# Linear attention with routed experts on one core: projections regrouped, normalisation spread over three engines, ranks and register loads in new places

## The chip, the core and the metric

The kernel runs on one NeuronCore of a Trainium2 chip. The metric is the device time of one execution in microseconds, as the median of several executions. The core has TensorE (PE, matrix products, with its weight loads shown as PEld), VectorE (DVE), ScalarE (ACT), GpSimd (POOL) and SyncE (SP); each has its own instruction stream, runs it in order, and waits for others through semaphores.

## What is computed

The input `x` is 8 x 256 tokens of 128 features: 2048 tokens, 16 tiles of 128. The output is the input plus two branches over its layer norm:

```python
xn = (x - mean) / sqrt(var + 1e-5)
# branch 1: linear attention, 16 heads of 8 features, inside each batch of 256 tokens
Q, K, V = xn @ Wq, xn @ Wk, xn @ Wv
Qf, Kf = elu(Q) + 1, elu(K) + 1
out1 = (Qf @ (Kf.T @ V)) / (Qf @ sum(Kf) + 1e-6)   # per head
out1 = out1 @ Wo
# branch 2: top 2 of 8 experts for every token
probs = softmax(xn @ gate_w.T + gate_b)
out2 = sum over the two largest: probs[e] * (relu(xn @ w1[e] + b1[e]) @ w2[e] + b2[e])
x + out1 + out2
```

All is fp32. Each expert is 128 x 256 and 256 x 128.

## The kernel before, in words

The order of the work is written out by hand, as one list of steps for each engine; there is no scheduler. A *part* is a group of tiles that are loaded and normalised together (`PARTS`: tiles 0-1, 2-3, 4-7, 8-11, 12-15), a *block* is four tiles, a *batch* two tiles.

**Normalisation.** DVE takes the statistics of each part (`statistics`, L593), ACT the square root (`deviation`, L485), DVE the reciprocal (`inverse_deviation`, L601). The tiles themselves are normalised by DVE, ACT or POOL as `NORM_DVE`, `NORM_ACT` and `NORM_POOL` say (L103 to L105). PE transposes a part (`transpose_x`, L880), and ACT copies the result to SBUF (`copy_xT`, L500).

**Projections.** `project_kv` (L913) makes keys and values of one batch: a product of ones with one row, which adds 1 to the keys, two tiles of keys, two of values, in one PSUM bank, of which three take turns. ACT takes the exponential of the keys (`exp_k`) and copies the values (`copy_v`), DVE finishes the keys (`finish_k`, L726). `make_logits` (L897) makes the gate's logits of four tiles: a product of one row for the bias and four products of 8 columns. `project_q` (L950) makes queries of a block. An fp32 product of one tile is two matmul instructions in the profile, each with its own weight load.

**Ranks.** DVE finds the two best experts of each token in PSUM (`top_two`, L617), and which of the 28 pairs of experts they are (`find_pair`, L626). `rank_rows` (L932) counts on PE how many tokens of each pair come before; after the fourth, DVE makes each token's row number from it (`pair_starts`, `places`, L649 to L669), `slot_done` says so. POOL then writes every tile's rows to DRAM at these row numbers (`dispatch`, L429), sixteen indirect DMAs, each behind the gates of its rows (`gate_values` on POOL for tiles 0 to 7, `late_gates` on DVE for the others). SP reads the sorted rows back when all sixteen have landed (`load_rows`, L355). `visits`, `order_visits` and `make_table` turn the pair counts into a table of at most 59 visits, each of one expert to one tile of sorted rows.

**Attention.** `keys_values` (L972, into one PSUM bank), `mask_kv` (L739), `numerator` (L987), `divide` (L746), `transpose_att` (L1002), `project_out` (L1010) and `residual` (L763) run over the four blocks.

**Experts.** PE transposes the sorted rows (`transpose_rows`, L1023) and makes 59 visits: `first_product` (L1037), a relu on ACT (L538), `second_product` (L1054). DVE adds the bias (`take_y`, L773) and adds to the tile's sum (`accumulate`, L781). PE, DVE and SP read each visit's addresses from the table into registers, `LOADS` visits at a time, each by a TENSOR_LOAD (`offsets_of`, L328). POOL adds every finished tile to the output by an indirect DMA (`give_back`, L452), which waits for the number of visits that can reach the tile: 8, 16, 23, 28, 33, 37, 40, 43 for the first eight tiles and then two more for each.

## Time and profile before

| | |
|---|---|
| median of three executions | 121.21 us (121.0 to 124.61) |
| the profiled execution, its own time | 120.49 us |
| its span in the profile | 118.7 us |
| mean granted TensorE clock | 0.938 of full speed |
| busy: PE, PEld, DVE, ACT, POOL | 105.1, 94.5, 70.9, 58.6, 48.6 us |

The span is the time from the first to the last instruction; about 1.8 us of the execution's time lie around it. PE busy counts a matmul from its start to its modelled end, and these overlap, so the distance between starts is the better measure of cost. "issue" as a releaser means that the engine waited for nothing that the profile shows.

### The profile page before, as it was taken

The page shows a single profiled execution, that of the slowest core. Times are in us where ns is not written, and L with a number is a line of the kernel's source. Part 1 is how long each engine was busy: PE and PEld are TensorE (multiplying, and loading weights), DVE is VectorE, ACT ScalarE, POOL GpSimd, SP SyncE. Part 2 cuts the span into 40 slices and gives each one's busy share as a digit, 9 for nine tenths or more (in the row PEclk, how much of TensorE's full clock was granted, in tenths as well). Part 3 has the DMA queues.
Part 4 walks back from the last instruction along what each step waited for, and adds up shares of the span by engine and source line. Part 5 has one row for each costly group of instructions (what it writes and reads, how often), then busy time and mean ns, then how long its engine had stood idle before and what let it go on. Part 6 is the DMA issues. An engine that isn't in the chain of part 4 may idle for free.

```text
span 118.7 us, 3131 instructions
## 1 busy us (share of the span) xinstructions
PE 105.1 (89%) x787; PEld 94.5 (80%) x787; DVE 70.9 (60%) x292; ACT 58.6 (49%) x169; POOL 48.6 (41%) x62
## 2 busy tenths in 40 slices
PE   6969799999999999777999999999999999999200
PEld 6957677565768799666999999999999999999100
DVE  0878953949717478943376665656657566575510
ACT  1556945232245203214866677766766776666000
POOL 5004221007777778411000500405405556878770
PEclk9999999755599999999999999999999999999975
DMA  3997000000211851499675575766776777883422
GB/s 93 289 370 315 3 6 0 0 0 24 71 50 50 223 165 57 105 239 315 186 182 136 136 160 145 168 162 144 171 166 151 166 183 170 140 161 34 42 25 25
DMA packets 16514, 15.51 MB, mean 131 GB/s; under 512 B 1778, under 2 KB 16114, under 8 KB 16370
## 3 DMA queue, kind: packets, MB, share of 16 engines
q1 hardware_dynamic: 13248, 12.88, 38.3%
q0 software_dynamic: 2816, 2.18, 12.3%
q10 hardware_dynamic: 434, 0.27, 0.7%
q8 instruction: 7, 0.11, 0.4%
q14 instruction: 9, 0.07, 0.2%
HBM read 12.09 MB, written 3.23 MB: 129 GB/s over the span
## 4 chain that ended last, share of the span: by engine, by line
PE 36%; issue 28%; POOL 19%; ACT 4%; DVE 3%; DVEq 2%; POOLq 2%; DMA 2%
POOL out L457 19%; PE banks L960 4%; PE banks L925 4%; PE banks L983 4%; PE banks L877 4%; PE banks L998 3%; PE banks L928 3%; PE banks L909 2%; PE banks L1019 2%; DVEq L330 2%; DMA out<-res 2%; ACT xrow L497 2%; POOLq L115 2%; ACT xT L503 2%; PE banks L893 1%
## 5 line engine op out<-in xcount | busy, mean ns | idle before, releaser
L543 ACT ACTIVATE h<-banks,w_now 128x128 f32<-128x128 f32 x118 | 36.9, 365 | 17.6 <-PE banks L1050 17.6
L457 POOL DMA_INDIRECT out<-acc,token x16 | 25.1, 1569 | 34.3 <-DVE acc L786 33.1
L1050 PE MATMUL banks<-xsT,w_now 128*128 x236 | 36.4, 278 | 0.7 <-ACT xsT L536 0.7
L1063 PE MATMUL banks<-w_all,h 128*128 x236 | 36.1, 277 | 0.0
L1050 PEld LDWEIGHTS banks<-xsT,w_now 128*128 128x128 f32 x236 | 30.9, 192 | 1.2 <-issue 1.1
L1063 PEld LDWEIGHTS banks<-w_all,h 128*128 128x128 f32 x236 | 31.0, 192 | 0.3
L778 DVE TENSOR_TENSOR y<-banks,w_all 128x128 f32<-128x128 f32 x59 | 17.2, 292 | 20.7 <-DVE acc L786 11.3
L786 DVE SCALAR_TENSOR_TENSOR acc<-y,xs,acc 128x128 f32 x59 | 20.7, 351 | 0.8 <-DVE y L778 0.6
L442 POOL DMA_INDIRECT sorted_dram<-xrow,slot x16 | 15.5, 971 | 10.4 <-DVE slot L669 6.1
L531 ACT COPY attT<-banks 128x512 f32<-128x512 f32 x4 | 2.3, 586 | 9.1 <-PE banks L1007 9.1
L526 ACT ACTIVATE qf<-banks,minus_one 128x512 f32<-128x512 f32 x4 | 2.8, 688 | 8.2 <-PE banks L960 8.2
L925 PE MATMUL banks<-wkvg_f,xT 128*128 128x128 f32 x32 | 6.7, 341 | 0.0
L521 ACT ACTIVATE kf<-banks,minus_one 128x256 f32<-128x256 f32 x8 | 3.8, 473 | 4.7 <-PE banks L928 4.7
L925 PEld LDWEIGHTS banks<-wkvg_f,xT 128*128 128x128 f32 x32 | 5.0, 223 | 1.2 <-issue 0.4
L928 PE MATMUL banks<-wkvg_f,xT 128*128 128x128 f32 x32 | 5.8, 312 | 0.0
L1019 PE MATMUL banks<-wo_f,attT 128*128 128x128 f32 x32 | 4.4, 280 | 1.5 <-ACT attT L531 1.5
L596 DVE BATCH_NORM_STATS2 stats<-x_tok 128x6 f32<-128x128 f32 x16 | 3.6, 281 | 3.5 <-DMA x_tok<-in_x 3.5
L983 PEld LDWEIGHTS banks<-vext,kf 128*128 128x128 f32 x32 | 5.2, 227 | 0.5 <-issue 0.5
L983 PE MATMUL banks<-vext,kf 128*128 128x144 f32 x32 | 5.6, 326 | 0.0
L877 PE MATMUL banks<-ones 128*128 128x128 f32 x22 | 4.6, 399 | 1.1 <-POOL ones L385 1.1
L960 PE MATMUL banks<-xT,wq_f 128*128 128x512 f32 x8 | 5.5, 769 | 0.0
L1019 PEld LDWEIGHTS banks<-wo_f,attT 128*128 128x128 f32 x32 | 3.9, 191 | 1.9 <-DVE res L765 1.9
(100 smaller groups left out, 117.3 us busy)
## 6 DMA issues: line engine op xcount, KB each, us to landing
w_now<-in_w1b SPq DMA_DIRECT2D x59, 129.0 KB, 2.6
w_all<-in_w SPq DMA_DIRECT2D x1, 1536.0 KB, 8.4
out<-res SPq DMA_DIRECT2D x4, 256.0 KB, 4.5
xs<-sorted_dram SPq DMA_DIRECT2D x3, 276.0 KB, 5.2
x_tok<-in_x SPq DMA_DIRECT2D x3, 256.0 KB, 4.7
xs<-sorted_dram SPq DMA_DIRECT2D x2, 138.0 KB, 2.3
x_tok<-in_x SPq DMA_DIRECT2D x2, 128.0 KB, 2.5
sorted_dram<-xrow,slot POOLq DMA_INDIRECT x16, 2.4
```

The costliest lines, as they stand in the source:

```text
L442: nc.gpsimd.indirect_dma_start(out=sorted_dram, out_offset=bass.IndirectOffsetOnAxis(ap=slot[:, t:t + 1], axis=0), in_=xrow[:, t, :], in_o ...
L457: nc.gpsimd.indirect_dma_start(out=out_rows, out_offset=bass.IndirectOffsetOnAxis(ap=token[:, s:s + 1], axis=0), in_=acc[:, s * D:(s + 1) ...
L543: nc.scalar.activation(h[:, i % NH, c, :], h_ps[i % NHP][:, c * P:(c + 1) * P], ACT.Relu, bias=w1_now[:, i % NW, H + c:H + c + 1]).then_in ...
L778: nc.vector.tensor_tensor(y[:, i % 2, :], y_ps[i % NYP], w2_all[:, bass.ds(woff + KC * D, D)], ALU.add).then_inc(y_done, 1)
L786: nc.vector.scalar_tensor_tensor(out=mine, in0=y[:, i % 2, :], scalar=xs[:, bass.ds(goff, 1)], in1=mine, op0=ALU.mult, op1=ALU.add).then_i ...
L925: nc.tensor.matmul(kvp_ps[b][:, r, 0:D], xT[:, (R * b + r) * P:(R * b + r + 1) * P], wkvg_f[:, 0:D], start=False, stop=(r == R - 1))
L928: last = nc.tensor.matmul(kvp_ps[b][:, r, D:KV], xT[:, (R * b + r) * P:(R * b + r + 1) * P], wkvg_f[:, D:KV], start=True, stop=True)
L960: nc.tensor.matmul(q_ps[k], wq_f[:], xT[:, blk_cols(k)], start=False, stop=True).then_inc(q_done, 1)
L983: last = nc.tensor.matmul(kv_ps[:, 256 * b:256 * b + NV], kf[:, t, :], vext[:, t, :], start=(r == 0), stop=(r == 1))
L1019: last = nc.tensor.matmul(wo_ps[k][:, j * P:(j + 1) * P], attT[:, t * P:(t + 1) * P], wo_f[:], start=True, stop=True)
L1050: last = nc.tensor.matmul(h_ps[i % NHP][:, c * P:(c + 1) * P], w1_now[:, i % NW, c * P:(c + 1) * P], xsT[:, bass.ds(toff, P)], start=True, ...
L1063: last = nc.tensor.matmul(y_ps[i % NYP], h[:, i % NH, c, :], w2_all[:, bass.ds(woff + c * D, D)], start=(c == 0), stop=(c == KC - 1))
```

## The change

- Logits leave their own products. `project_vg` multiplies a tile of xT by the columns of V and of the gate together (136 columns); a bank holds two tiles, and four banks take turns. The one-row product for the gate's bias is gone: DVE adds the bias when it copies the logits to SBUF (`take_logits`), for two tiles at a time, and the bias is loaded to all partitions. `top_two` now works on two tiles and reads SBUF.
- Keys are made for four tiles at a time (`project_k`, one bank), and `exp_k` and `finish_k` take four tiles in one instruction.
- Normalisation: DVE has one tile less in parts 2 and 4, POOL takes tiles 7 and 15; `statistics(3)` and `(4)` stand before the part ahead of them is finished.
- The list of every engine is new: on DVE all pairs are found ahead of `shares`, `finish_k` and the late gates; on PE the rank products stand between the value products, and attention's steps are reordered after `numerator(1)`; ACT switches to the exponential's table after `copy_v(3)`.
- `LOADS` is 10 instead of 8, and PE's first two register loads stand before `project_out(2)` and `project_out(3)`.

```diff
-    LOADS, AHEAD = 8, 3
+    LOADS, AHEAD = 10, 3
...
-    NORM_DVE = [[0, 1], [2], [4, 5], [], [12, 13]]
-    NORM_ACT = [[], [3], [6, 7], [8, 9], [14, 15]]
-    NORM_POOL = [[], [], [], [10, 11], []]
+    NORM_DVE = [[0, 1], [2], [4], [], [12]]
+    NORM_ACT = [[], [3], [5, 6], [8, 9], [13, 14]]
+    NORM_POOL = [[], [], [7], [10, 11], [15]]
...
-        q_ps = [banks[:, (k + 1) % 2, :] for k in range(NBLK)]
-        kvp_ps = [banks[:, 2 + b % 3, :].rearrange("p (r n) -> p r n", r=R) for b in range(B)]
+        q_ps = [banks[:, i, :] for i in (2, 3, 4, 2)]
+        vg_ps = [banks[:, (2, 3, 4, 6)[b % 4], 0:R * (D + E)].rearrange("p (r n) -> p r n", r=R) for b in range(B)]
+        k_ps = [banks[:, i, :].rearrange("p (t d) -> p t d", t=4) for i in (7, 1, 0, 7)]
...
+            normalise(2)
             normalise(3)
+            normalise(4)
             fill_rows()
...
-            nc.scalar.dma_start(gate_bias[:], gate_b).then_inc(gate_b_in, 16)
+            nc.scalar.dma_start(gate_bias[:], gate_b.partition_broadcast(P)).then_inc(gate_b_in, 16)
...
             deviation(2)
+            normalise(2)
+            deviation(3)
+            normalise(3)
+            copy_xT(2)
+            deviation(4)
             copy_v(0)
-            deviation(3)
-            normalise(2)
-            normalise(3)
-            deviation(4)
-            copy_xT(2)
+            normalise(4)
+            copy_xT(3)
             copy_v(1)
+            copy_xT(4)
+            copy_v(2)
+            copy_v(3)
             exponentials()
-            copy_xT(3)
-            normalise(4)
+            exp_gates(0)
+            exp_gates(1)
+            for b in range(4, B):
+                copy_v(b)
             exp_k(0)
-            exp_gates(0)
-            copy_xT(4)
             exp_k(1)
...
+            def take_logits(b):
+                ts = slice(R * b, R * b + R)
+                dve.wait_ge(vg_done, b + 1)
+                if b == 0:
+                    dve.wait_ge(gate_b_in, 16)
+                nc.vector.tensor_tensor(logits[:, ts, :], vg_ps[b][:, :, D:D + E],
+                                        gate_bias[:].unsqueeze(1).to_broadcast([P, R, E]), ALU.add
+                                        ).then_inc(logits_done, 1)
...
+            def project_vg(b):
+
+                if b == 0:
                     pe.wait_ge(wkvg_in, 16)
+                pe.wait_ge(xT_copied, parts_with(R * b + 1))
+                if b >= 4:
+                    pe.wait_ge(v_done, b - 3)
+                for r in range(R):
+                    last = nc.tensor.matmul(vg_ps[b][:, r, :], xT[:, (R * b + r) * P:(R * b + r + 1) * P],
+                                            wkvg_f[:, D:KVG], start=True, stop=True)
+                last.then_inc(vg_done, 1)
+
+            def project_k(k):
+
+                if k == 0:
+                    pe.wait_ge(ones_set, 2)
+                elif k < 3:
+                    pe.wait_ge(xT_copied, k + 3)
+                else:
+                    pe.wait_ge(kf_done, 1)
+                nc.tensor.matmul(k_ps[k], ones_bf[0:1, 0:P], ones_bf[0:1, :].rearrange("p (t d) -> p t d", t=4),
                                  start=True, stop=False)
                 for j in range(4):
+                    t = 4 * k + j
+                    last = nc.tensor.matmul(k_ps[k][:, j, :], xT[:, t * P:(t + 1) * P], wkvg_f[:, 0:D],
                                             start=False, stop=(j == 3))
+                last.then_inc(k_done, 1)
...
```

The new lists of steps after the change, DVE from the statistics of part 3 on, then PE:

```
DVE: statistics(3), inverse_deviation(2), normalise(2), statistics(4), inverse_deviation(3),
     take_logits(0), top_two(0), inverse_deviation(4), normalise(4), take_logits(1), top_two(1),
     find_pair(0), take_logits(2), top_two(2), choose(0), take_logits(3), top_two(3), find_pair(1),
     (take_logits, top_two)(4), (5), find_pair(2), (take_logits, top_two)(6), (7), find_pair(3),
     shares(0), choose(1), shares(1), choose(2), pair_starts, places(1), places(2), late_shift,
     choose(3), finish_k(0), late_gates, finish_k(1), finish_q(0), finish_k(2), visits, finish_k(3),
     order_visits, finish_q(1), keep_table, mask_kv(0), finish_q(2), finish_q(3), mask_kv(1),
     mask_kv(2), divide(0), mask_kv(3), ... as before
PE:  warm_up, transpose_x(0), (1), project_vg(0), (1), project_k(0), transpose_x(2),
     project_vg(2), (3), transpose_x(3), rank_rows(0), project_vg(4), transpose_x(4),
     project_vg(5), rank_rows(1), project_vg(6), (7), project_k(1), rank_rows(2), project_q(0),
     rank_rows(3), project_k(2), project_q(1), (2), project_k(3), keys_values(0), order_visits,
     project_q(3), make_table, keys_values(1), (2), numerator(0), (1), transpose_att(0),
     keys_values(3), project_out(0), transpose_att(1), numerator(2), project_out(1), numerator(3),
     transpose_att(2), register load, project_out(2), transpose_att(3), register load,
     project_out(3), then the experts
```

In the PE list of before, `keys_values(3)` stood ahead of `transpose_att(0)`, and `numerator(2)` ahead of `project_out(0)` and `transpose_att(1)`.

## Rows read from the trace of the kernel before

**Rows 1.** The chain in order of time, steps of PE: start, us, what

```profile
14.61 0.69 PE banks L944 x4
...
19.55 0.99 PE banks L909 x8
...
32.55 1.05 PE banks L960 x2
...
34.46 0.45 PE banks L928 x4
...
37.82 0.98 PE banks L983 x8
38.80 0.32 PE banks L959
```

**Rows 2.** Timeline, 53 to 55 us: the first visit

```profile
53.86 0.37 ACT L536 COPY xsT<-banks 128x256 f32<-128x256 f32 x1 [1.53 <-PE banks L1033]
...
54.71 1.15 PE L1050 MATMUL banks<-xsT,w_now 128*128 x8 [0.67 <-ACT xsT L536]
```

**Rows 3.** Timeline: the rows' way through DRAM, POOL, SP's queue, POOL

```profile
26.77 1.15 POOL L442 DMA_INDIRECT sorted_dram<-xrow,slot  x1 [5.83 <-DVE slot L669]
...
48.21 2.51 SPq L357 DMA_DIRECT2D xs<-sorted_dram  x5
...
50.56 0.18 POOL L449 CAST token<-xs 128x2 uint32<-128x2 f32 x1 [1.87 <-DMA xs<-sorted_dram]
```

**Rows 4.** Timeline, 85 to 114 us, the visits on DVE and PE, POOL's writes

```profile
85.77 0.29 DVE L778 TENSOR_TENSOR y<-banks,w_all 128x128 f32<-128x128 f32 x1 [0.49 <-DVE acc L786]
...
92.98 0.29 DVE L778 TENSOR_TENSOR y<-banks,w_all 128x128 f32<-128x128 f32 x1 [0.49 <-DVE acc L786]
...
96.26 0.61 PE L1063 MATMUL banks<-w_all,h 128*128 x4
...
97.86 0.29 DVE L778 TENSOR_TENSOR y<-banks,w_all 128x128 f32<-128x128 f32 x1 [0.21 <-PE banks L1063]
...
98.73 1.55 POOL L457 DMA_INDIRECT out<-acc,token  x1 [0.83 <-DVE acc L786]
...
113.88 1.55 POOL L457 DMA_INDIRECT out<-acc,token  x1 [0.30 <-issue]
```

**Rows 5.** The page's second part: TensorE's granted clock in 40 slices, in tenths

```profile
PEclk9999999755599999999999999999999999999975
```

**Rows 6.** Windows: length, busy us of PE, PEld, DVE, ACT, POOL, clock, DMA share, GB/s

```profile
18.00:22.00 4.00, 3.78 (x24) 2.32 (x23) 2.30 (x20) 1.76 (x6) 0.75 (x3) 1.00 0.00 0
...
28.00:32.00 4.00, 4.00 (x17) 3.65 (x16) 3.62 (x13) 1.31 (x3) 2.89 (x3) 0.50 0.16 53
```

**Rows 7.** Timeline, 10 to 16 us: POOL's scaling, a copy of xT, DVE's searches

```profile
10.46 0.61 POOL L394 TENSOR_TENSOR xrow<-x_tok,mean_var 128x256 f32<-128x256 f32 x1 [8.27 <-DVE rstd L604]
...
11.87 0.56 ACT L503 COPY xT<-banks 128x512 f32<-128x512 f32 x1
...
14.10 0.38 DVE L620 MAX8 top<-banks 128x8 f32<-128x8 f32 x4
...
15.08 0.17 DVE L632 TENSOR_SCALAR idxk<-idx 128x8 f32<-128x8 uint32 x1
```

**Rows 8.** Timeline, 25 to 30 us, DVE: the ranks and what follows

```profile
25.35 0.21 DVE L653 TENSOR_TENSOR_SCAN start_of<-ones,banks 128x28 f32<-128x28 f32 x1 [1.50 <-PE banks L944]
...
27.47 0.50 DVE L669 TENSOR_REDUCE slot<-picked 128x12 uint32<-128x336 f32 x1
27.89 0.21 DVE L710 TENSOR_REDUCE expsum<-expd 128x8 f32<-128x64 f32 x1
...
29.05 0.68 DVE L736 SCALAR_TENSOR_TENSOR qf<-qf,banks 128x512 f32<-128x512 f32 x1
```

**Rows 9.** Timeline, 42 us, DVE: the first division begins

```profile
42.17 0.23 DVE L750 TENSOR_SCALAR den<-banks 128x64 f32<-128x64 f32 x1 [0.18 <-PE banks L998]
```

**Rows 10.** Register loads, line 330, PE's queue: count, ns min/median/max, first and last start

```profile
L330 PEldq TENSOR_LOAD <-table x16: 587/592/1649, 52.8 to 107.6; - x16
```

More of the change, by code:

```diff
@@ L154, in linear_attention_with_pair_sorted_experts @@
         res = sb("res", [P, T, D])
+        logits = sb("logits", [P, T, E])
         top8 = sb("top8", [P, T, 8])
@@ L207, in linear_attention_with_pair_sorted_experts @@
         table_ps = banks[0:3, 5, P:P + NI]
-        logits_ps = [banks[:, 6 + g % 2, 0:4 * E].rearrange("p (t e) -> p t e", e=E) for g in range(NBLK)]
         kv_ps = banks[:, 6, :]
@@ L514, in copy_v, with exp_k @@
             def copy_v(b):
[L515 to L521 removed]
+                act.wait_ge(logits_done, b + 1)
+                nc.scalar.copy(vext[:, R * b:R * b + R, 0:D], vg_ps[b][:, :, 0:D]).then_inc(v_done, 1)
+            def exp_k(k):
+                act.wait_ge(k_done, k + 1)
+                nc.scalar.activation(kf[:, blk_tiles(k), :], k_ps[k], ACT.Exp, bias=minus_one[:, 0:1]
                                      ).then_inc(kexp_done, 1)
@@ L795, in _ @@
             statistics(2)
+            statistics(3)
             inverse_deviation(2)
             normalise(2)
-            statistics(3)
+            statistics(4)
             inverse_deviation(3)
-            statistics(4)
+            take_logits(0)
             top_two(0)
-            find_pair(0)
             inverse_deviation(4)
             normalise(4)
+            take_logits(1)
+            top_two(1)
+            find_pair(0)
+            take_logits(2)
+            top_two(2)
             choose(0)
-            top_two(1)
+            take_logits(3)
+            top_two(3)
             find_pair(1)
+            take_logits(4)
+            top_two(4)
+            take_logits(5)
+            top_two(5)
+            find_pair(2)
+            take_logits(6)
+            top_two(6)
+            take_logits(7)
+            top_two(7)
+            find_pair(3)
+            shares(0)
             choose(1)
-            shares(0)
-            finish_k(0)
             shares(1)
-            finish_k(1)
-            top_two(2)
-            find_pair(2)
             choose(2)
-            top_two(3)
-            find_pair(3)
-            late_shift()
-            choose(3)
             pair_starts()
@@ L822, in _ @@
             places(2, slice(4, T))
+            late_shift()
+            choose(3)
+            finish_k(0)
             late_gates()
+            finish_k(1)
             finish_q(0)
@@ L827, in _ @@
             finish_k(3)
+            order_visits()
             finish_q(1)
-            order_visits()
-            finish_k(4)
+            keep_table()
             mask_kv(0)
-            keep_table()
-            finish_k(5)
             finish_q(2)
-            finish_k(6)
+            finish_q(3)
             mask_kv(1)
-            finish_k(7)
-            finish_q(3)
             mask_kv(2)
@@ L1100, in _ @@
             numerator(1)
+            transpose_att(0)
             keys_values(3)
-            transpose_att(0)
-            numerator(2)
             project_out(0)
             transpose_att(1)
+            numerator(2)
+            project_out(1)
             numerator(3)
-            project_out(1)
             transpose_att(2)
+            toffs = offsets_of(mybir.EngineType.PE, 1, 0, T_TOP)
             project_out(2)
             transpose_att(3)
+            woffs = offsets_of(mybir.EngineType.PE, 0, 0, W_TOP)
             project_out(3)
```

134 lines of the change are left out of this document (46 added, 88 removed).

## The prediction, made before the changed kernel was built

> **What bounds the kernel now.** I read the chain of waits in order of time first. Up to 5.7 us it is TensorE's warm-up, then normalising and ACT's copies of xT alternate; from about 12.5 us to the end of attention nearly every piece is a product on TensorE [rows 1]. After that, "issue" and POOL's additions alternate: the experts run on TensorE at 0.89 us a visit, and the chain ends on POOL. The first visit's product starts at 54.71 us, 0.85 us after ACT has begun its copy of the sorted rows; that copy needs 0.37 us, so about 0.45 us are the register load in front [rows 2]. The other way to the first visit goes through DRAM: POOL's sixteen writes start at 26.77 us, the read is issued at 48.21, and POOL holds the first rows at 50.56 us [rows 3]. TensorE came to transposing them only after 53.3 us, so this way has some 2.8 us to spare, and attention sets the start. What moves the start of the visits moves the end as much, for the 59 visits are there in both. In the tail DVE lags: the bias addition of visit 43 starts at 97.86 us, though TensorE's product for it was over about 1.15 us earlier (the product at 96.26 and 0.45 us), and from the eighth write on POOL is nearly back to back, 15.15 us for 8 writes [rows 4]. Last, the clock: it falls to half at about 22.2 us and is back at about 32.4 [rows 5, 6], ten microseconds in which TensorE is the chain.
>
> **The change on TensorE.** Removed: four one-row products (0.32 us each by the like one of the queries) and 32 passes of 8 columns, 0.99 us for eight; that is 4 x 1.31 = 5.2 us [rows 1]. A batch's values and logits are four passes of 136 columns. They lie between four of 128 in 0.45 us and, of 144, eight in 0.98 us: 0.45 to 0.49, I take 0.47 [rows 1]. Keys of a block are a one-row product of 512 columns, 0.32, and eight passes, 0.89: 1.2 us, against 2 x 0.65 before.
>
> One rule speaks against a gain here. The 8-column pass takes 0.12 us, as much as one of 128 columns [rows 1]. The Trainium skill (TensorE: Matmul & The Clock Gate, Back-to-back issue gap) lets a small matmul's gap sink to about 25 ns, but says for pairs with a weight load that both instructions set the spacing. By the floor alone the 32 passes would give back, as an estimate, only 0.8 us instead of 4; the trace agrees with the second half of the rule.
>
> **Step 1, up to the ranks.** `statistics(3)` ahead of part 2's scaling delays that scaling by 0.6 us, but DVE has one tile less, and ACT takes its tiles of part 2 before it waits for part 3's deviation: part 2 is normalised at about 9.8 us instead of 11.0. ACT then does part 3's two tiles and copies xT of part 2. That copy began at 11.87 us [rows 7]; now about 11.45, and the next products start at 12.0. POOL's single tiles in parts 2 and 4 were not traced: two operations of 128 columns each, between half of the one of 256 columns and all of it, so 0.6 to 1.2 us [rows 7]. I take 0.7, which lies inside ACT's two tiles (0.88) and costs nothing; at 1.2 it costs 0.3. From 12.0 to the end of the last rank product TensorE has six value products, 2.8; eight transposes, 0.9; four rank groups of about 0.7 [rows 1], 2.8; keys of one block, 1.2; queries of one block, 0.32 + 1.05, 1.4: 9.1 us. One wait: `rank_rows(0)` needs the first pairs, and TensorE's next products and part 4's transposes are queued behind it. On DVE the first pairs follow the deviation of part 4 (12.25, behind ACT's copy), 0.65 us of scaling, one batch's logits, and the pair: 14.3 us, where TensorE is free at 13.4: 0.9 us. Sum: 12.0 + 9.1 + 0.9 = 22.0 us, against 25.3 before (the scan that waited for it starts at 25.35 [rows 8]): 3.3 us earlier.
>
> DVE in this stretch has more to do. Eight `take_logits` were not traced either; the nearest small operations take 0.17 us [rows 7] and 0.21 [rows 8], so 0.2 each with its handover. `top_two` and its searches take 0.98 us for four tiles [rows 7]; as two pairs 1.06, from SBUF perhaps 0.1 less. So 0.7 us a batch, 1.7 us more over all. From 14.3 on DVE's own sum (six batches 4.2, three pairs 2.1, a `choose` 0.2, then both `shares` and two `choose` 1.1) ends at 21.9 us, level with TensorE. An error of 0.1 us a batch therefore costs up to 0.8 us. ACT: the table load moves from an idle stretch (12.7 us) behind `copy_v(3)`; loaded with its first use in 1.5 us, values 4 to 7 follow to 21.0, `project_q(0)` needs value 4 at about 19.9 and starts at 20.2. Hidden, with 0.3 us of cover. The bias's broadcast load is a different access on ACT's queue; all loads of this size landed within 5 us, it is read at 10.6 us: hidden.
>
> **Step 2, ranks to the first division.** This stretch becomes DVE's. In order: scan and both places 2.65 (25.35 to 27.97 [rows 8]); late shift and choice 0.35; late gates 1.25 (27.89 to the finish at 29.05 and its overlap); four `finish_k` of 512 columns and four `finish_q`, 0.65 each at the spacing behind a row of 0.68 [rows 8], 5.2; visits 0.95; order and table 1.0, a wait of 0.2 in it; two masks 0.8. Sum 12.2, to 34.2 us. TensorE's second `keys_values` waits for `keep_table` and the first mask, but its 0.98 us lies beside `finish_q`. Behind 34.2 come `keys_values(2)` and `numerator(0)`, 0.98 each [rows 1]: the first division starts at 36.1 us against 42.17 [rows 9]: 6.1 earlier, 2.8 more than step 1 gave, much of it the clock, which I leave at full here. `order_visits` on TensorE waits for DVE's visits (29.8), and `project_q(3)` stands behind it; still in time for `finish_q(3)` at 33.0.
>
> POOL's first write, after one `places` (1.15) and handover, starts at 23.5, the whole way is 3.3 us earlier [rows 3]; POOL's own gates for blocks 0 and 1 follow `shares` at 21.3 and end at 23.3, just in time. The first rows are there at 47.3 us.
>
> **Step 3, the divisions.** It gives something back. `keys_values(3)` now stands behind `transpose_att(0)`, which waits for the first division, and DVE's next step, `mask_kv(3)`, waits for it: 0.44 + 0.98 + 0.05 = 1.5 us instead of 0.4. `numerator(2)` stands behind `transpose_att(1)`: DVE waits 0.9 us more where it waited for nothing. The first register load, 1.65 us where its kind takes 0.59 [rows 10], lies behind `transpose_att(2)`, beside ACT's copy of 0.6: it costs between 0 and 0.6 us. I take 12.6 us from first division to the last product's end, where 11.2 stood: 1.4 us lost, with 0.9 and 2.0 as ends. Attention ends at 48.7 us, 1.4 us after the first rows are there.
>
> **Step 4, the first visit.** Without the register load in front it follows ACT's copy at once, 0.95 us behind attention's end instead of 1.35: 0.4 us gained [rows 2]. It starts at 36.1 + 12.6 + 0.95 = 49.65 us, 5.1 earlier. DVE's three loads are ten values each now, not traced; their length for eight is the same few tenths whatever the line, and they lie beside TensorE's first two visits. Between nothing and 0.3 us.
>
> **Step 5, the visits.** DVE's cycle with 8 visits is 85.77 to 92.98, 7.21 us [rows 4]: five visits of 0.80 and three of 1.075, each of these with one register load in it. TensorE's eight are 7.15. So DVE never catches up. With 10 it is seven of 0.80 and three of 1.075, 8.8, against 8.93: the lag of 1.15 us at visit 43 should shrink to about 0.3, and POOL starts its closing run 0.8 earlier. The run itself has 1.55 + 0.30 us a write [rows 4], 14.8 at best against 15.15. I take 0.9 us for both, 0.3 to 1.2 as ends. The rest is worth nothing, for POOL holds the end.
>
> **The sum.** -3.3 - 2.8 + 1.4 - 0.4 - 0.9 = -6.0 us at full clock. The last unknown is the clock.
>
> **The clock.** It fell, from 2.4 to 1.2 GHz, after a stretch with TensorE at work 3.78 of 4 us, in short passes, with weight loads busy 2.32 us, and it came back after one with weight loads for 3.65 us [rows 6]. The change makes 14 to 22 us denser, but between 8.5 and 12 us TensorE has only 0.85 us of keys and 0.44 of transposes, less than in the stretch that ended in the fall. So I expect a fall again, at about 12 us, now followed by dense work, and so shorter. While it lasts each 0.111 us pass costs 0.22, but the wait for the first pairs takes up the first microsecond. A slow stretch of 3.4 to 7 us costs 1.0 to 2.2; I take 1.2. Result: 120.49 - 6.0 + 1.2 = 115.7 for the profiled execution, and since the median was 0.7 above that execution, 116.4 us.
>
> The Trainium skill (TensorE: Matmul & The Clock Gate, Why this matters for your kernels) ties a fall to TensorE standing idle between bursts. No idle gap stood before this fall, so the trace doesn't agree. By the rule alone the changed kernel, whose longest gap is 1.75 us, would not fall; that is rival A.
>
> **Rivals.** A: the clock stays up. For it: the empty passes of 8 columns are gone, and 14 to 22 us is dense. Against it: the thin stretch before 12 us. 120.49 - 6.0 + 0.7 = 115.2 us. B: the clock is down as long as before, 10 us from 12 to 22. Then only half of step 1's 9.1 us is done in it: the ranks end 4.2 us later, at 26.1, and everything behind. 119.4 us. For it: the same length before [rows 5]. C: attention is quicker than I add up and the rows' way binds: visits start at 47.3 + 0.95 = 48.25, 1.4 earlier still, and the time is 113.8. Against it: 1.4 us of spare. D, slower: the clock falls twice, at 12 and again in the divisions (34 to 46 us), where every step of TensorE is on the chain: `keys_values(2)` and (3), two numerators, three transposes, some 5 us at full clock. That costs 4.2 + 4.7 against 6.0, so 124.1 us; it decides from about 6 us of loss on, some 14 slow microseconds in places that TensorE bounds. For it: DVE's stretch of step 2 leaves TensorE idle 3 to 4 us of 28 to 35. Against it: no fall in the like divisions of before [rows 5].
>
> **Chances.** Forecast 0.42, its own range 115.3 to 117.9; A 0.25; B 0.17; C 0.08; D 0.08. The range 114.4 to 119.8 leaves out C, D and little else. 2% of 121.21 are 2.4 us, about what a measurement here tells from no change: below 118.8 lie the forecast, A, C and a part of B, 0.80; within 2% the rest of B and of the near cases, 0.13; above, 0.07.
>
> **What would show it.** Right: no products of 8 columns; the scan after the ranks near 22 to 23.5 us; the first division near 37; DVE idle some 1.5 us ahead of the fourth mask; the first visit at 50 to 51 us with no "issue" in front; DVE close behind TensorE at visit 43. Wrong: a slow clock beyond 20 us, DVE late with the fourth pair, the first visit after 53 us, or the first rows later than attention's end.

## The result and the profile after

The changed kernel takes 137.51 us (136.91 to 138.33, 4 runs), the kernel before in the same session 121.1 (119.86 to 124.61, 4 runs): ratio 1.140, 95% interval 1.127 to 1.153, slower. The forecast was 116.4, range 114.4 to 119.8, with a chance of 0.07 for slower. The profiled execution took 138.33 us, where the working came to 115.7; its span is 136.5. The kernel before has medians of 123.91, 124.36 and 121.48 us in the sessions of the experiments, since some executions there, of the changed versions too, had a lower mean clock; the ratios leave those out.

| us of the span | forecast | before | after |
|---|---|---|---|
| scan behind the ranks | 22.0 (clock aside) | 25.35 | 23.46 |
| first division | 36.1 (clock aside) | 42.17 | 40.67 |
| first rows on POOL | 47.3 | 50.56 | 49.69 |
| first visit's product | 50.85 with 1.2 for the clock | 54.71 | 55.99 |
| from there to the end of the span | 63.1 | 64.0 | 80.5 |

By the second last row 5.1 us of the miss of 22.6 had come up before the visits, by the last 17.4 in them. (The first rows came 2.4 us later than forecast, but TensorE was not waiting for them.) The visits do what they did before and their lines are as short as before, so the first question is what stands between them. DVE's timeline, columns start, length, engine, line, operation, operands, and in brackets the idle time ahead with its releaser:

```profile
64.48 0.29 DVE L786 TENSOR_TENSOR y<-banks,w_all 128x128 f32<-128x128 f32 x1 [0.21 <-DVE acc L794]
...
68.08 0.29 DVE L786 TENSOR_TENSOR y<-banks,w_all 128x128 f32<-128x128 f32 x1 [2.19 <-PE banks L1072]
...
70.87 0.29 DVE L786 TENSOR_TENSOR y<-banks,w_all 128x128 f32<-128x128 f32 x1 [2.20 <-issue]
...
73.68 0.29 DVE L786 TENSOR_TENSOR y<-banks,w_all 128x128 f32<-128x128 f32 x1 [2.23 <-PE banks L1072]
...
92.60 0.29 DVE L786 TENSOR_TENSOR y<-banks,w_all 128x128 f32<-128x128 f32 x1 [2.19 <-PE banks L1072]
```

Three visits in a row have 2.2 us of nothing ahead of their bias addition, where [rows 4] had 0.49. The same three stalls begin again at 92.60, twenty visits later: 24.52 us for twenty, 1.23 a visit, against 7.21 for eight, 0.90, before. The releaser in the bracket names TensorE twice, but only because its product came last before a long gap. What DVE does in it is in the chain of waits:

```profile
64.71 0.46 PE banks L1072 x4
65.89 1.97 DVEq L332
68.67 1.98 DVEq L332
71.45 2.00 DVEq L332
74.21 0.71 PE banks L1072 x4
```

DVEq is DVE's sequencer, L332 the register load. TensorE has gaps of its own there:

```profile
66.72 0.71 PE L1059 MATMUL banks<-xsT,w_now 128*128 x4 [1.56 <-issue]
...
70.98 0.71 PE L1072 MATMUL banks<-w_all,h 128*128 x4 [1.34 <-issue]
```

And the view of one source line, L332, by queue (count, shortest, median and longest in ns):

```profile
L332 DVEq TENSOR_LOAD <-table x18: 1059/2078/2407, 52.0 to 120.1; - x18
L332 PEldq TENSOR_LOAD <-table x12: 1078/2279/2453, 49.4 to 116.7; - x12
L332 SPq TENSOR_LOAD <-table x6: 953/1514/2091, 33.1 to 108.7; - x6
```

Before, TensorE's had a median of 592 ns [rows 10]. Ten values cost not 10/8 of that but 1.06 to 1.08 us in one half of the loads and 2.0 to 2.45 in the other. In order of time they alternate: the groups that begin at visit 0, 20 and 40 are the short ones, those at 10, 30 and 50 (nine values) the long ones. The group at visit 0 is an exception: its first loads on TensorE took 1.28 and 2.41 us, DVE's first 2.41.

Ahead of the visits these first loads show: TensorE's last output product starts 1.67 us late behind its load of 2.41 us, and DVE's last residual stands 4.05 us behind its first three. TensorE's two in one line of the view:

```profile
L332 PEldq TENSOR_LOAD <-table x2: 1277/1844/2411, 49.4 to 51.5; - x2
```
```profile
54.03 1.13 PE L1028 MATMUL banks<-wo_f,attT 128*128 128x128 f32 x8 [1.67 <-issue]
```
```profile
56.70 0.69 DVE L773 TENSOR_TENSOR res<-banks,x_tok 128x512 f32<-128x512 f32 x1 [4.05 <-issue]
```

The clock fell before the visits as well, and twice, where before there was one stretch [rows 5]. The page's second part, and windows of 4 us (columns as in [rows 6]):

```profile
PEclk9999599999559999999999999995999999599995
```
```profile
14.00:18.00 4.00, 4.00 (x24) 3.16 (x24) 3.60 (x31) 1.15 (x4) 0.95 (x7) 0.68 0.00 0
...
34.00:38.00 4.00, 3.36 (x14) 3.04 (x14) 1.11 (x3) 0.00 (x0) 3.03 (x4) 0.50 0.62 145
38.00:42.00 4.00, 3.61 (x20) 3.39 (x18) 1.72 (x5) 0.00 (x0) 3.08 (x4) 0.69 0.52 173
```

The second stretch lies in `keys_values(1)` and (2) and the first numerators, where nearly every step of TensorE is on the chain. The later dips, at 92 and 116 us, come behind the gaps that the long loads leave.

Theory R, from here on: the register loads make the loss of the visits, and a load is long where its values begin on a column that isn't a multiple of four. The 2.41 us above don't fit it, for that load begins on column 0; in other versions too an engine's first loads take longer than later ones of the same size (up to 1.65 us before, 1.25 on TensorE in e1, 1.97 in e11), and no run shows why. One rival: a load is long when it holds more than eight values, wherever it begins. Another: the loads only cover a wait of another kind (the clock, the new order), and the visits would be slow with short loads too.

### The profile page after: what moved, and what is told of

The parts are those of the page before. It is cut to its first block, busy times and chain, and to the rows that moved or that the text cites. A ratio compares the mean times of both kernels' runs of the same rounds, so it can differ in the third digit from the quotient of the medians.

```text
span 136.5 us, 3023 instructions
## 1 busy us (share of the span) xinstructions
PE 106.4 (78%) x743; PEld 94.6 (69%) x743; DVE 71.8 (53%) x294; ACT 57.5 (42%) x165; POOL 50.5 (37%) x66
## 3 DMA queue, kind: packets, MB, share of 16 engines
q0 software_dynamic: 2816, 2.18, 10.9%
## 4 chain that ended last, share of the span: by engine, by line
PE 58%; DVE 13%; issue 9%; DVEq 5%; DMA 4%; ACT 4%; POOL 2%; POOLq 1%; SPq 1%
PE banks L1059 19%; PE banks L1072 18%; DVEq L332 4%; PE banks L990 4%; DMA x_tok<-in_x 4%; PE banks L921 3%; PE banks L1005 3%; PE banks L1028 2%; DVE stats L597 2%; ACT h L547 2%; POOL out L459 2%; PE banks L1014 2%; DVE acc L794 2%; PE banks L968 2%; PE banks L953 1%
## 5 line engine op out<-in xcount | busy, mean ns | idle before, releaser
L547 ACT ACTIVATE h<-banks,w_now 128x128 f32<-128x128 f32 x118 | 36.9, 365 | 33.2 <-PE banks L1059 33.0
L1059 PE MATMUL banks<-xsT,w_now 128*128 x236 | 38.5, 288 | 7.0 <-issue 6.0
L1072 PE MATMUL banks<-w_all,h 128*128 x236 | 38.4, 288 | 3.8 <-issue 2.2
L1059 PEld LDWEIGHTS banks<-xsT,w_now 128*128 128x128 f32 x236 | 32.7, 201 | 8.2 <-issue 8.2
L1072 PEld LDWEIGHTS banks<-w_all,h 128*128 128x128 f32 x236 | 32.5, 200 | 5.5 <-issue 5.5
L990 PE MATMUL banks<-vext,kf 128*128 128x144 f32 x32 | 6.8, 374 | 1.5 <-DVE kv L749 1.5
L921 PE MATMUL banks<-wkvg_f,xT 128*128 128x136 f32 x32 | 5.6, 315 | 1.5 <-ACT xT L507 1.5
L893 PEld LDWEIGHTS banks<-ones 128*128 128x128 f32 x22 | 4.8, 331 | 1.1 <-POOL ones L387 1.1
L1005 PE MATMUL banks<-kv,qf 128*128 128x144 f32 x32 | 5.4, 325 | 0.0
L773 DVE TENSOR_TENSOR res<-banks,x_tok 128x512 f32<-128x512 f32 x4 | 2.7, 686 | 4.6 <-issue 4.0
L1005 PEld LDWEIGHTS banks<-kv,qf 128*128 128x128 f32 x32 | 5.2, 230 | 0.0
```

The source lines that it names most:

```text
L547: nc.scalar.activation(h[:, i % NH, c, :], h_ps[i % NHP][:, c * P:(c + 1) * P], ACT.Relu, bias=w1_now[:, i % NW, H + c:H + c + 1]).then_in ...
L893: last = nc.tensor.matmul(warm_ps, ones[:], ones[:], start=True, stop=True)
L921: last = nc.tensor.matmul(vg_ps[b][:, r, :], xT[:, (R * b + r) * P:(R * b + r + 1) * P], wkvg_f[:, D:KVG], start=True, stop=True)
L990: last = nc.tensor.matmul(kv_ps[:, 256 * b:256 * b + NV], kf[:, t, :], vext[:, t, :], start=(r == 0), stop=(r == 1))
L1005: last = nc.tensor.matmul(num_ps[k][:, j // 2, (j % 2) * NV:(j % 2 + 1) * NV], qf[:, t * P:(t + 1) * P], kv[:, t // 2, :], start=True, sto ...
L1059: last = nc.tensor.matmul(h_ps[i % NHP][:, c * P:(c + 1) * P], w1_now[:, i % NW, c * P:(c + 1) * P], xsT[:, bass.ds(toff, P)], start=True, ...
```

## The experiments

**Eight values again, all else as changed (e1), and ten values in the kernel before (e2).**

```
-    LOADS, AHEAD = 10, 3
+    LOADS, AHEAD = 8, 3        # e1, in the changed kernel; e2 is 8 to 10 in the kernel before
```

> The changed kernel with one edit taken back: 8 values per register load instead of 10. Theory R (a load costs by its values and by where it begins: eight that begin on a multiple of four are taken together in 0.59 us, every other value alone in about 0.23 us): all loads are back to 0.59 us, the visits take the 64 us from the first product to the span's end that they took before, and the first product comes about 1 to 1.5 us earlier than the 55.99 of the changed kernel, since the load of 2.41 us in front of the last output product shrinks; some 118.5 to 120.5 us in all. Rival F (the new order of the front is what costs): still above 130 us.

> The kernel before with 10 values per register load and nothing else of the change. Theory R: loads of 1.07 and 2.3 us by turns, and the visits take the 80.5 us from first product to the end that they take in the changed kernel, 16.5 more than before: 136 to 139 us. Rival F: within 2 us of the kernel before.

e1: 120.61 us (118.63 to 121.45), ratio 0.988 (0.947 to 1.028). e2: 139.45 (136.07 to 142.38), the kernel before beside it 123.91. From the first product to the end of the span e1 takes 64.3 us, e2 80.5 (58.5 to 139.0), the changed kernel's own figure. So this one constant makes 16.2 us of the visits' loss, in either kernel, and no wait of another kind is needed. e2's time lies just above the 136 to 139 expected. The line of the loads in e1, then in e2:

```profile
L332 PEldq TENSOR_LOAD <-table x16: 588/595/1245, 49.3 to 108.1; - x16
```
```profile
L330 PEldq TENSOR_LOAD <-table x12: 1077/2256/2449, 56.0 to 119.5; - x12
```

**The place, with the count kept (e3), and the count, with the place mended (e4).** e3 is the kernel before, eight values a load, the table moved by two columns. e4 is the changed kernel with ten values a load, each group on a column that is a multiple of twelve; DVE's copy of the table is two operations instead of one.

```
 e3:     table = sb("table", [3, NI + 2], I32)
...
-             table[row:row + 1, i:min(i + LOADS, NI)], ...
+             table[row:row + 1, i + 2:min(i + LOADS, NI) + 2], ...
 e4:     PITCH = 12
...
-             table[row:row + 1, i:min(i + LOADS, NI)], ...
+             table[row:row + 1, i // LOADS * PITCH:i // LOADS * PITCH + min(LOADS, NI - i)], ...
```

> The kernel before, 8 values per load, but the table begins two columns later, so that every load begins at 2 modulo 8 columns. Theory R: no eight lie together from a multiple of four, so each load is eight single values, about 1.85 us instead of 0.59; three loads on VectorE per eight visits cost 1.26 us more each, seven times over: some 20 to 25 us more, 141 to 146 us. Rival L (it is the count: beyond eight values a load falls to a slow way, wherever it begins): 0.59 us and 121 us as before.

> The changed kernel with 10 values per load, but each group of ten begins at a multiple of twelve columns of the table, so always on a multiple of four. Theory R: every load of ten is about 1.07 us, none 2.3; the three groups that had 2.3 us lose 3 x 1.25 us each on VectorE, so 10 to 12 us less than the changed kernel, 125 to 128 us. Rival L: no change against the changed kernel, 137 us.

e3: 146.39 us (146.16 to 149.2), ratio 1.211 (1.172 to 1.249). e4: 122.84 (122.44 to 125.98), ratio 1.017 (0.982 to 1.051). The loads of e3, then of e4:

```profile
L330 DVEq TENSOR_LOAD <-table x24: 742/1844/3127, 50.2 to 135.2; - x24
```
```profile
L333 DVEq TENSOR_LOAD <-table x18: 857/1064/1677, 48.3 to 105.6; - x18
L333 PEldq TENSOR_LOAD <-table x12: 854/1082/1280, 45.6 to 103.5; - x12
```

Eight values take 1.84 us where they begin two columns off, three times their 0.59; ten on a good column take 1.06, and none takes 2 us. Both missed their expected times: e3 lies 0.4 us above 146, and e4 is 14.7 us under the changed kernel where 10 to 12 were expected. The rule of more than eight falls, R stands. In e3 1.84 / 8 is 0.23 us a value; its groups of three, the shortest, took 0.74, 0.25 a value. But R was not complete: with good columns for all, the visits of e4 still take 69.2 us (51.36 to 120.6), 4.9 more than those of e1.

**Twelve values (e8).** This tells whether the good load goes by single values or in steps.

```
-    LOADS, AHEAD = 10, 3
+    LOADS, AHEAD = 12, 3
```

> The changed kernel with 12 values per load; every group begins on a multiple of four. Theory R leaves open how the quick way is cut. If it takes four values at a time: 3 x 0.30 = 0.9 us for twelve. If it takes eight and then single values: 0.59 + 4 x 0.23 = 1.5 us. If it needed a multiple of eight at the start: three of the five groups quick, two slow with 2.8 us. The time: 118 to 122 us in the first case, 123 to 127 in the second, above 128 in the third.

121.01 us (120.37 to 123.62), ratio 1.006 (0.998 to 1.014).

```profile
L332 DVEq TENSOR_LOAD <-table x15: 843/858/1535, 48.2 to 101.0; - x15
L332 PEldq TENSOR_LOAD <-table x10: 849/864/1330, 45.6 to 99.1; - x10
```

Twelve values take 0.86 us, less than ten (1.07) and as long as nine (0.86, the last groups of e4). Eight are 0.59: so the times are those of fours at some 0.29 us each, and what is left over costs about 0.24 a value: ten is 2 x 0.29 + 2 x 0.24 = 1.06. From a column off the fours the cost is that of single values: 10 x 0.23 = 2.3. The twelves begin on columns 0, 12, 24, 36 and 48, so a multiple of eight isn't needed. All slow groups here begin two columns past a multiple of four; an odd column was not tried.

With these lengths DVE's cycle can be added up as in the prediction, where a load of 0.59 made a visit 0.275 longer than 0.80, 0.32 less than its own length. Twelve values: 12 x 0.80 + 3 x 0.54 = 11.2 us, against 10.7 of TensorE, 2.5 us over the visits; measured (67.2 - 64.3) 2.9. Ten on good columns: 8.0 + 3 x 0.75 = 10.25 against 8.93 for ten visits, 7.8 us over all; measured 4.9. The cycle itself came as added up: DVE's loads of e4 start at 61.3 and, forty visits later, at 102.8, 10.4 us for ten. The base was too low: in e1 they go from 62.8 to 107.4 in 48 visits, 9.3 for ten and not 8.93. Ten as changed: three short loads and three long ones in twenty visits, 16 + 3 x 0.75 + 3 x 1.98 = 24.2; measured 24.52.

**Which engine's loads (e11, e12).** TensorE has ten values a load in e11 and eight in e12, DVE and SP the other number.

```
+    PE_LOADS = 10              # e11, with LOADS = 8; e12: 8, with LOADS = 10
...
-             table[row:row + 1, i:min(i + LOADS, NI)], ...
+             table[row:row + 1, i:min(i + (PE_LOADS if engine == mybir.EngineType.PE else LOADS), NI)], ...
```

> The changed kernel with ten values a load on TensorE, eight on DVE and SP. From the measured lengths TensorE's loads in the visits add up to 6 x 2.4 + 4 x 1.08 = 18.7 us instead of 14 x 0.59 = 8.3: 10.4 more. Theory R (the sequencer of each engine stands for its own load, and the engine with more to do bounds): 59 visits of 0.89 and 18.7 are 71.2 us, about 74.5 from the first product to the end of the span, where e1 has 64.3 and the changed kernel 80.5; the time is some 131 us. Rival: the loads cost on DVE alone, and this kernel is as fast as e1, 120 to 121 us.

> The changed kernel with ten values a load on DVE and SP, eight on TensorE. DVE's loads add up to about 9 x 2.2 + 6 x 1.07 = 26.2 us instead of 21 x 0.59 = 12.4. Theory R: 59 visits of 0.80 and 26.2 are 73.4 us, with the tail of 4 about 77 to 78 from the first product to the end of the span; about 134 us. Rival: the loads cost on TensorE alone, and this kernel is as fast as e1, 120 to 121 us. If the costs of the two engines simply added, e11 and e12 together would be 88 - 64 = 24 us over e1; the changed kernel is only 16 over it, so each alone must be over half of that.

e11: 134.36 us, e12: 139.19, one run each. From the first product to the end of the span 76.1 and 86.1. Over e1's 64.3 TensorE's loads alone cost 11.8 us and those of DVE with SP's 21.8, and the two don't add: both together, in the changed kernel, cost 16.2. e11's visits came near what Theory R had (74.5); its time is 3.4 us over the 131 expected, about half of it because its first visit starts at 56.54 us, 1.6 later than e1's (part 2 of x, tiles 4 to 7, came 1.1 us later there). e12 is 8 us over its 78. Its waits show why: while DVE stands for three loads in three visits TensorE, whose banks it hasn't read, stands too, and the clock falls; after that TensorE is late. Rows of e12, TensorE's timeline and two windows:

```profile
71.13 0.71 PE L1073 MATMUL banks<-w_all,h 128*128 x4 [1.64 <-DVE y L787]
...
73.27 1.06 PE L1073 MATMUL banks<-w_all,h 128*128 x4
```
```profile
68.00:72.00 4.00, 1.87 (x12) 1.50 (x12) 1.55 (x6) 1.28 (x4) 0.00 (x0) 1.00 0.62 124
72.00:76.00 4.00, 3.74 (x19) 3.75 (x20) 1.75 (x6) 1.25 (x4) 0.00 (x0) 0.57 0.15 38
```

A sum per engine is therefore a floor of the loss, not the loss. How the 8 us divide between the clock and the waiting was not taken apart. Against the changed kernel e12, with less to load, has 5.6 us more in the visits; its page has four slices at half clock in them before the last one, against two there. Two more slices of 3.4 us at half clock are, as an estimate, at most 3.4 us of the 5.6; the rest is open, and each has one profile here.

**The order of the divisions (e6).** On top of e1 the old order: `keys_values(3)` ahead of `transpose_att(0)`, `numerator(2)` ahead of `project_out(0)`, `numerator(3)` ahead of `project_out(1)`.

```
+            keys_values(3)
             transpose_att(0)
-            keys_values(3)
+            numerator(2)
             project_out(0)
             transpose_att(1)
-            numerator(2)
+            numerator(3)
             project_out(1)
-            numerator(3)
```

> The changed kernel with 8 values per load and, behind the second numerator, TensorE's steps in the order of before: the fourth keys_values ahead of the first transpose, the third numerator ahead of the first output product. Theory (as the prediction had it, 0.9 to 2.0 us lost by the new order): VectorE waits about 0.4 us instead of 1.7 for the fourth mask and not at all instead of 1.1 us for the third division; first division to last output product 1.5 to 2 us shorter, 1 to 2 us less in all than the same kernel in the new order. Rival: the waits move elsewhere in the stretch and nothing is gained.

118.97 us (118.33 to 119.88), ratio 0.991 (0.980 to 1.002). From the first division to the first visit e1 took 14.39 us (40.57 to 54.96), e6 12.26 (40.72 to 52.98): 2.1 less. The fourth mask waited 1.73 us in the changed kernel and 0.36 in e6, rows of the one and of the other:

```profile
44.00 0.46 DVE L749 TENSOR_TENSOR kv<-banks,cst 128x288 f32<-128x288 f32 x1 [1.73 <-PE banks L990]
...
47.69 0.23 DVE L758 TENSOR_SCALAR den<-banks 128x64 f32<-128x64 f32 x1 [1.13 <-PE banks L1005]
```
```profile
42.68 0.46 DVE L749 TENSOR_TENSOR kv<-banks,cst 128x288 f32<-128x288 f32 x1 [0.36 <-PE banks L990]
...
45.62 0.21 DVE L758 TENSOR_SCALAR den<-banks 128x64 f32<-128x64 f32 x1
```

**TensorE's first two loads, moved out of the end of attention (e9).** On top of e6 they stand behind `keys_values(1)` and `keys_values(2)`.

```
             keys_values(1)
+            toffs = offsets_of(mybir.EngineType.PE, 1, 0, T_TOP)
             keys_values(2)
+            woffs = offsets_of(mybir.EngineType.PE, 0, 0, W_TOP)
...
             transpose_att(2)
-            toffs = offsets_of(mybir.EngineType.PE, 1, 0, T_TOP)
             project_out(2)
             transpose_att(3)
-            woffs = offsets_of(mybir.EngineType.PE, 0, 0, W_TOP)
             project_out(3)
```

> The changed kernel with eight values a load and the old order of the divisions (as e6), and TensorE's two first register loads moved to behind the second and the third of its key-value products, where it waits for DVE's masks. In e6 these loads stood in the last two steps of attention: TensorE's product of output rows 2 began 0.76 us behind ACT's copy, product 3 likewise, and output 1 to output 3 took 4.8 us from the start of one to the start of the other (46.23 to 51.02). Theory S (the loads stand beside ACT's copy and cost only what is longer than it): output 1 to output 3 shortens by 0.2 to 0.9 us, first division to first visit from 12.26 to some 11.6 us, and the first division comes no later than in e6 if the loads fit into TensorE's idle time ahead of it (0.6 to 1 us there, at 0.6 to 1.65 us a load: they may cost up to 1 us). Rival: the cover is complete, the interval stays at 12.2 to 12.3, and the first division comes up to 1 us later: 119 to 120 us. By Theory S the median is 118.5, range 117.5 to 119.5.

119.46 us (117.8 to 120.24), ratio 0.981 (0.968 to 0.994); beside e6 no difference that these runs can tell. The two output products still wait 0.77 us each for ACT's copy, and division to visit takes 12.58 us. The rival holds: with eight values the loads lie wholly beside the copy, and moving them gave nothing; the first division came no later for it either (40.56 us, 40.72 in e6). Only the load of 2.41 us stuck out of the copy.

```profile
48.85 1.13 PE L1028 MATMUL banks<-wo_f,attT 128*128 128x128 f32 x8 [0.77 <-ACT attT L535]
...
51.19 1.13 PE L1028 MATMUL banks<-wo_f,attT 128*128 128x128 f32 x8 [0.77 <-ACT attT L535]
```

**The clock (e5, e10).** e5 is e1 with 25 products of ones in TensorE's waits, into banks that the next product overwrites; they compute nothing that is used.

```
+            fill(5, 6)
...
+            fill(5, 2)
...
+            pe.wait_ge(kf_done, 2)
+            fill(1, 4)
...
+            fill(1, 3)
...
+            fill(1, 3)
...
+            fill(4, 3)
...
+            fill(4, 4)
```

> The changed kernel with 8 values per load and idle places of TensorE before the first visit filled with products of ones by ones into free banks (25 of them, 0.22 us each at full clock, 5.6 us in all, which compute nothing that is used). Theory: the clock falls in the thin stretches that the change made, and filled stretches keep it up: no slow stretch before the visits, the scan behind the ranks at 22.5, the first division at 37 instead of 40.6 us, the first visit near 51 instead of 55, 116 to 118 us. Rival: the falls come whatever TensorE does, and the fill only delays it: slow stretches as in the unfilled kernel and 121 us or more.

118.65 us (117.79 to 119.87), ratio 0.986 (0.978 to 0.994). The first stretch of 1.2 GHz came all the same, against the theory, the second didn't, and the time lies above the 116 to 118 expected:

```profile
12.00:16.00 4.00, 4.00 (x23) 4.00 (x24) 2.85 (x25) 2.72 (x8) 2.65 (x9) 0.61 0.09 36
34.00:38.00 4.00, 4.00 (x32) 3.75 (x32) 2.33 (x6) 0.55 (x1) 3.06 (x4) 1.00 0.47 141
38.00:42.00 4.00, 3.95 (x34) 3.76 (x33) 1.94 (x5) 0.59 (x1) 3.09 (x4) 1.00 0.61 178
```

e10 is this fill on top of e9, without its last two places: 18 products, not the 25 that its expectation names.

> e9 with the 25 products of ones in TensorE's waits (they compute nothing that is used), as in e5. If e5's gain against e1 (2 us by the medians) came from the clock that stayed up in the divisions, the same comes on top of e6's order, and the median is 117 to 118 us, with no slow stretch beyond 20 us; the visits last 64 to 65 us from the first product to the end of the span as in every version with eight values. Rival: e5 was luck of the clock, or the fill delays real products as much as the clock gives: 118.5 to 120 us.

118.32 us (117.84 to 119.48), ratio 0.984 (0.973 to 0.995), against 137.51 of the change as it was and 121.48 of the kernel before in that session. No slow stretch before the tail. The first division starts at 37.15 us, and TensorE comes to the first visit's rows when they have just landed. It stands for 0.18 us; the profile names no releaser, but POOL's first operation, which waits for the same load, starts within 0.04 us of it:

```profile
48.73 0.19 POOL L451 CAST token<-xs 128x2 uint32<-128x2 f32 x1 [1.90 <-DMA xs<-sorted_dram]
```
```profile
48.77 0.93 PE L1046 MATMUL banks<-ident,xs 128*128 128x128 f32 x4 [0.18 <-issue]
49.78 1.15 PE L1063 MATMUL banks<-xsT,w_now 128*128 x8
...
56.50 0.71 PE L1063 MATMUL banks<-xsT,w_now 128*128 x4 [1.03 <-DMA w_now<-in_w1b]
```

From there the visits of e10 take 66.2 us (49.78 to 116.0), where 64 to 65 were expected; those of e9 take 65.2. In e10 TensorE waits 1.03 us for the weights of a visit, the last row above. So an earlier start of the visits isn't handed on whole here, and the time lies just over the 117 to 118 expected.

What the fill gives in time isn't settled: the intervals of e9 and e10 overlap nearly whole, and the clock also stayed up in the profiles of e4, e7, e8 and e12, which have no fill. On the clock itself the fill has an effect: the mean clock over the span was 0.979 to 0.985 in all four runs of e10, and 0.933 to 0.949 in all four of e9 beside them. Without any edit the clock differs too: one run of e1 took 118.63 us at a mean clock of 0.986, another 120.1 at 0.952. The profiles show the stages. The first division starts at 40.56 to 40.72 us in e1, e6, e9 and the changed kernel, in which the clock fell twice, and at 36.87 to 37.53 in e4, e7, e8, e10 and e12, in which it didn't fall before the visits: about 3.7 us, of which up to 0.4 can be x, whose part 2 came 0.2 to 0.4 us later in the first four than in e4. (e11 fell twice too and had part 2 later still: 41.66.) In every profile of the changed kernel's front without fill that had the first fall the second followed, and in none without the first.

**The bias's load (e7).** On top of e1 the broadcast load of the gates' bias stands as the last of ACT's loads, behind its second square root, instead of among the first.

> The changed kernel with 8 values per load and the load of the gate's bias issued by ScalarE behind its second square root, near 5 us, instead of among the first loads. Theory: the 128 small pieces of the bias load stand in the way of x's third part, which lands near 7.2 us instead of 6.2: it lands again near 6.2, part 2 is transposed at 9.8 instead of 10.8 us, and up to 0.9 us are gained. Rival: that part lands when it lands (5.9 to 6.8 us in three profiles of the old front), and nothing moves.

119.82 us (117.98 to 120.6), ratio 0.987 (0.966 to 1.009). The gain didn't come. DVE's statistics of part 2 of x start at 6.79 us here, at 6.85 to 7.38 in eight of the versions with the load in its early place (8.49 in e5 and e11, 6.16 before): 0.1 to 0.6 us earlier and not near the 6.2 expected. The edit has a price instead: issued at 4.8 us, the bias lands 8.0 us later (4.9 in its early place in e4), and DVE's first logits wait for it. They start at 12.84 us, 11.00 in e4:

```profile
12.84 0.17 DVE L623 TENSOR_TENSOR logits<-banks,gate_bias 128x16 f32<-128x16 f32 x1 [1.92 <-DMA gate_bias<-in_gate_b]
```

With the clock up in both, the scan starts at 23.29 us against 22.45 in e4, the first division at 37.53 against 36.94. Why part 2 of x comes later than before stays open.

## Why the prediction was wrong

**The step that failed is the price of the register load, in steps 4 and 5.** The prediction said of the ten-value loads: "their length for eight is the same few tenths whatever the line", and "with 10 it is seven of 0.80 and three of 1.075". It kept the price of a load and cut their number. Measured, the three were 0.48 us longer each on a good column and 1.7 on a bad one, so ten of DVE's visits took 12.3 us (24.52 for twenty) where 8.8 stood, and the lag grew instead of shrinking. That makes 16.2 of the 22.6 us by e1, which differs from the changed kernel in that number alone. The trace of before had a warning, for its shortest group, three values in about 0.75 us, was longer than eight in 0.59:

```profile
L330 DVEq TENSOR_LOAD <-table x3: 743/756/759, 106.9 to 109.4; - x3
```

A price that falls with more values isn't a fixed one, and a bound of "between nothing and 0.3 us" for an operation that no row showed was no bound.

The Trainium skill (Runtime: NRT & Kernel Launch, Instruction fetch mechanics) gives about 200 ns for each register of a TENSOR_LOAD, where it speaks of loads from HBM; these read SBUF. An estimate from it is 2.0 us for ten values and 1.6 for eight. The traces come near it for the loads off a multiple of four (0.23 us a value) and not for those on one (0.59 for eight, in the trace of before already). The Trainium skill (DMA: Bandwidth & Descriptors, Latency and other measured facts) gives a `tensor_load` floor of some 600 ns. The traces have 0.59 us for eight values on DVE and TensorE and 0.53 on SP, and the length goes on growing with the count.

**Steps 1 and 2 had the right chain, and came out 0.84 us short.** With the clock up (e4, e8) the scan starts at 22.45 and 22.49 against 22.0, the first division at 36.94 and 36.87 against 36.1. The chain that I added up is the one that is there; each sum was some 0.4 us short. For step 1 e4 shows where: ACT's copy of xT, forecast for 11.45 us, starts at 12.00, since part 2 of x comes at 6.96 us where it came at 6.16 before.

**Step 3 had the right mechanism, and the term was too small.** The fourth mask waits 1.7 us (forecast 1.5), the third numerator 1.13 (0.9). The order costs 2.1 us, not 1.4, just beyond the end of 2.0; the register load beside ACT's copy cost nothing with eight values and about 0.9 with ten as changed (15.3 us from division to visit against 14.4 in e1 and e4); this one is a first load on a good column, so its length isn't explained.

**Step 4.** Taking the load from the front of the visits was to give 0.4; e6, with the old order and eight values, has 12.26 us from division to visit against 12.54 before: 0.3. TensorE's gap ahead of the first visit's product was 0.67 us before and is 0.39 without the load.

**Step 5's gain of 0.9 us** hung on ten values at the price of eight, which no run had. The nearest is e8, twelve values in 0.86 us: its visits take 67.2 us, where e1, e5, e6 and e7 with eight take 64.2 to 64.8, and before 64.0. Of the 17.4 us missed in the visits 16.2 are the long loads, 0.9 this gain, and 0.3 the difference of e1 from before.

**The clock: forecast one fall for 1.2 us, came two for 3.7.** Rival D was right on the place of the second (34 to 46 us was forecast, 34 to 41 measured) and on its being worse than the first: up to the scan the changed kernel lost 1.0 us against e4, from there to the first division 2.7. Its reason was met in part: TensorE was idle 1.7 of the 7 us from 28 to 35, not 3 to 4. D was wrong on the price of both together, 8.9. Rival A, no fall, is what five of the ten experiments on the changed kernel showed, one of them filled. The forecast, the falls taken as they were, is thus 2.5 us short here, some 0.2 of them x's part 2.

These terms make the 5.1 us ahead of the visits: 0.84 of steps 1 and 2, 0.86 of steps 3 and 4, 0.9 of the long load in attention's end, 2.5 of the clock. With the clock up the first division does come 5.3 us earlier (36.9 against 42.17); in the changed kernel's profile the clock, the order and the long load had taken all of it back by the first visit.

No rival of mine had the mechanism that decided. D had the sign, for another reason.

## What to carry to other kernels

Price a register load by its columns, not as one instruction: groups of a multiple of four values, beginning on a multiple of four. Of the sizes tried here on good columns eight was the fastest (64.3 us of visits, twelve 67.2, ten 69.2). An edit that changes the size of something "fixed" gets a row for the new size, or a bound wide enough to change the sign. When a sum per engine says that two engines have equal work in a loop, a stall in either stops both, and its price must be taken from the loop with the stall in it.

## What the runs showed of the hardware that was not expected

- A register load takes about 0.29 us for four values that begin on a multiple of four columns (of 4 bytes), about 0.24 for each value left over, and 0.23 for each value where it begins two columns past one. Eight: 0.59 or 1.84. Ten: 1.07 or 2.0 to 2.45. Twelve: 0.86. These are DVE's and TensorE's; on SP's queue it is the same picture, 0.06 to 0.2 us shorter. An engine's first loads can be longer (0.8 to 2.4 us for those on good columns), and no run shows why.
- More values can be cheaper: twelve take 0.2 us less than ten.
- The second fall of the clock, at about 34 us, came with no idle gap of TensorE over 1 us ahead of it. Thin work doesn't tell the falls apart either: in the changed kernel TensorE was busy 2.34 us of the four from 30 to 34, but e4, whose clock stayed up, had 2.11 of four at 29 to 33 (e8 2.18 there, e7 2.51 at 30 to 34). What does go with it in the profiles without fill is the first fall; why stays open. Rows of the changed kernel and of e4:

```profile
30.00:34.00 4.00, 2.34 (x9) 1.20 (x10) 3.42 (x12) 0.69 (x1) 2.87 (x3) 0.95 0.17 55
```
```profile
29.00:33.00 4.00, 2.11 (x8) 0.96 (x9) 3.42 (x13) 0.69 (x1) 3.08 (x4) 1.00 0.18 55
```
